# A transformer layer's projections and FFN in 16-bit parts, with the FFN's first layer paired by weight block

## The chip, the cores and the metric

The kernel runs on one core of one Trainium2 chip. The metric is the device time of that core in microseconds (us), from the start of the program to its end; three runs of the kernel before gave 2216.15, 2221.99 and 2224.67, median 2221.99. The core has five engines with queues of their own: TensorE (PE; its weight loads are listed apart as PEld), VectorE (DVE), ScalarE (ACT), GpSimd (POOL) and SyncE (SP, which issues the DMAs here).

## The reference

Sixteen sequences of 512 tokens with 256 features go through two attention blocks and, after each of them, the same FFN; every block has a layer norm in front and a residual sum behind. All of it is float32.

```python
def _L0_ffn_ref(x, w_gate, w_up, w_down):
    wg, wu, wd = (w.astype(x.dtype) * (1.0 / 127.0) for w in (w_gate, w_up, w_down))
    gate = jnp.einsum('bsd,hd->bsh', x, wg)
    up = jnp.einsum('bsd,hd->bsh', x, wu)
    h = jax.nn.silu(gate) * up
    return jnp.einsum('bsh,dh->bsd', h, wd)

x = L0_attn_a_x                                   # [16, 512, 256]
x = x + _L0_attn_a_ref(_layernorm(x), Wq, bq, Wk, bk, Wv, bv, Wo, bo)   # 16 heads, window +-32 and 4 global tokens
x = x + _L0_ffn_ref(_layernorm(x), w_gate, w_up, w_down)                # 256 -> 768 -> 256
x = x + _L0_attn_b_ref(_layernorm(x), Wqkv, Wout, bout)                 # rotary scores over unrotated sum, causal
x = x + _L0_ffn_ref(_layernorm(x), w_gate, w_up, w_down)
```

The FFN's weights are integers from -127 to 127, stored as int32.

## The kernel before

**Precision.** Float32 products are made of two parts: a value x is split into a high part and the rest, and a product takes high times high, high times low and low times high. The projections and the FFN hold both parts as float32r, which TensorE takes in one pass. The FFN's integer weights are exact in one part, so an FFN product has two passes, one for each part of x or of h. The scores of both attentions are made from float16 parts already (`src_a`, `src_b`, `pack_a`, `pack_b`).

**Order.** There is no scheduler. A table `AT` gives every step of a sequence a place on a common line, every sequence q is moved by 425 q places, and all steps are sorted into `STEPS`. Each engine walks through `STEPS` and issues its share in that order, so that up to four sequences are interleaved on it: attention A of one, the first FFN (F1) and attention B (PB, RB, B) of others, the second FFN (F2) of the oldest. A step that waits holds everything behind it on its engine. The period of a sequence is about 129 us.

**The steps that the change touches**, with the lines of the profile:
- `turn_x` (L1027) transposes the normalised x on PE. ScalarE copies the result to the high part of `xT` (L1185), VectorE subtracts to get the low part (L1433).
- `qk_step` (L1081) makes q and k, transposed: 6 matmuls of 128x128 weights and 512 columns a step, 48 a sequence over both attentions. `v_step` (L1004) makes v: 12 matmuls of 256 columns a step, 48 a sequence; here a block of x is the stationary operand.
- The FFN of half a sequence goes over three pairs of hidden blocks, so a step index i runs from 0 to 5. `ffn_up` (L1053) makes gate (G) and up (U), 8 matmuls of 256 columns each: high part of x first (4 of them), then low part (4). ScalarE takes the tanh (L1196), VectorE finishes gate (L1440), multiplies by up (L1446) and rounds the high part of h (L1457), GpSimd subtracts for the low part of h (L1576), and `ffn_down` (L1069) adds 8 matmuls of 256 columns into `d_bank`. Over both FFNs that is 192 matmuls of L1053 and 96 of L1069 a sequence.
- `o_step` (L1017) is the output projection. Its two parts `on_parts` are float32r and lie in the tile `xT[0]`.

**Start.** Weights are loaded, transposed on PE (L754), split by VectorE (L1269, L1270) or copied out of PSUM by ScalarE (L1227, L1230) into staging places, from which three DMAs bring the FFN's weights to `w_g`, `w_u` and `w_d`; PE and ScalarE wait for them (`w_raw`). VectorE finds the largest FFN weight; if it is over 2048, PE takes a branch of its program with true float32 matmuls, which these inputs do not take.

Of the kernel before, what the change touches and what calls it, by code (L numbers as in the profile page):

```python
# [13 lines left out]
HID = 768  # L14
# [8 lines left out]
EXACT = 2048.0  # L23
# [283 lines left out]
def build(nc, x_in, Wq, bq, Wk, bk, Wv, bv, Wo, bo, Wqkv, Wout, bout, w_gate, w_up, w_down,  # L307
# [7 lines left out]
    with ctx:  # L315
# [7 lines left out]
        wa_qk = [sb(f"wa_qk{i}", [P, KT, 2 * D], F32R) for i in range(2)]  # L323
        wa_v = [sb(f"wa_v{i}", [P, KT, D], F32R) for i in range(2)]
        wa_o = [sb(f"wa_o{i}", [P, KT, D], F32R) for i in range(2)]
        wb_qk = [sb(f"wb_qk{i}", [P, KT, 2 * D], F32R) for i in range(2)]
        wb_v = [sb(f"wb_v{i}", [P, KT, D], F32R) for i in range(2)]
        wb_o = [sb(f"wb_o{i}", [P, KT, D], F32R) for i in range(2)]
        w_g = sb("w_g", [P, KT, HID], F32R)
        w_u = sb("w_u", [P, KT, HID], F32R)  # L330
        w_d = sb("w_d", [P, FT, D], F32R)
# [30 lines left out]
        xT = [[sb(f"xT{b}{i}", [P, KT, S], F32R) for i in range(2)] for b in range(2)]  # L362
# [6 lines left out]
        w_top, w_top1 = newton[:, 0:1], newton[0:1, 1:2]  # L369
# [42 lines left out]
        w_raw = sem("w_raw")  # L412
# [88 lines left out]
        st_dT = stage(st_probs, FT * D, FT, D)  # L501
# [24 lines left out]
        def _(sp):  # L526
# [25 lines left out]
            for n, (dst, a) in enumerate(((w_g, st_gT), (w_u, st_uT), (w_d, st_dT))):  # L552
                sp.wait_ge(w_staged, (4, 8, 11)[n])
                sp.dma_start(dst[:, :, :].bitcast(F32), a).then_inc(w_raw, 16)
# [29 lines left out]
            def load_b(rotated, j, q):  # L584
# [5 lines left out]
                if j >= 2:  # L590
                    sp.wait_ge(scores, q * units + units // GROUPS * (j - 1))
                elif q:
                    sp.wait_ge(scores, (q - 1) * units + units // GROUPS * (j + 3))
                elif j == 0 and not rotated:
                    sp.wait_ge(wb_split, 1)
                load_pack(pack_b[:, j % 2, rotated], src_b[:, rotated], j, (u_packed, r_packed)[rotated][j])
# [132 lines left out]
        def _(pe):  # L729
# [28 lines left out]
            pe.wait_ge(w_flag, 1)  # L758
# [272 lines left out]
            def plain(a, exact):  # L1031
                return a if exact else a.bitcast(F32)

# [7 lines left out]
            def ffn_up(block, i, up, part, q, exact):  # L1041
# [4 lines left out]
                if part == 0:  # L1046
                    gu("GU"[up], i, block, q)
                for k in range(KT):
                    if i == 0 and not up:
                        x_there(block, part, k, q)  # L1050
                    for f in range(2):
                        c = (2 * pair + f) * P
                        last = pe.matmul(bank[:, f * D:(f + 1) * D], plain(w[:, k, c:c + P], exact),  # L1053
# [631 lines left out]
```

## Time and profile before

| what | value |
|---|---|
| runs of the kernel | 2216.15 to 2224.67 us, median 2221.99 |
| profiled execution, first to last instruction (span) | 2225.3 us |
| device time of the profiled execution | not given apart; the span is what the rows are taken from |
| PE busy, weight loads busy | 1928.7 us (87%), 1388.2 us (62%) |
| ACT, DVE, POOL busy | 65%, 64%, 36% |
| mean granted TensorE clock | 0.939 of 2.4 GHz |

PE is the busiest engine. A matmul's recorded length (281 ns for one of 256 columns) is longer than the step from one to the next, because they are pipelined; the steps are read from the starts in the timeline. The granted clock is 1.0 or 0.5, that is 2.4 or 1.2 GHz.

### The profile page before, as it was taken

What the parts mean: (1) busy time and instruction counts of PE and PEld (TensorE: products, weight loads), DVE (VectorE), ACT (ScalarE), POOL (GpSimd) and SP (SyncE); (2) the same over time, 40 slices, a digit from 0 to 9 for tenths busy, and PEclk for the clock granted to TensorE, in tenths of its full rate; (3) what the DMA queues carried; (4) which work ended last, traced back from release to release, by engine and by line L of the source; (5) the groups of instructions that cost most, each with busy time, mean ns of one, the idle gap of its engine ahead of it and who ended that gap; (6) DMA issues with size and microseconds to landing.
All of it is one profiled execution on the core that took longest, in us unless ns stands there. A gap on an engine that the chain in (4) does not pass through costs nothing.

```text
span 2225.3 us, 63347 instructions
## 1 busy us (share of the span) xinstructions
PE 1928.7 (87%) x25221; PEld 1388.2 (62%) x25221; DVE 1422.0 (64%) x2971; ACT 1444.9 (65%) x3580; POOL 796.1 (36%) x1131
## 2 busy tenths in 40 slices
PE   5677889889898989989898998989899898989786
PEld 4463657666675766667576666757666675756545
DVE  5363667576676757667675765767576676765624
ACT  1227676676867677676767767676776867677580
POOL 0023243433424343442434344243434424344431
PEclk7788999999999999999999999999999999999886
DMA  7224344252435335243533424353342434333321
GB/s 190 72 44 97 62 111 100 78 107 81 106 68 126 85 84 108 77 106 64 126 85 87 105 82 100 67 126 85 86 106 76 111 70 120 81 95 86 73 61 35
DMA packets 129636, 201.87 MB, mean 91 GB/s; under 512 B 26768, under 2 KB 60560, under 8 KB 129312
## 3 DMA queue, kind: packets, MB, share of 16 engines
q1 hardware_dynamic: 129344, 197.80, 37.1%
q8 instruction: 205, 3.36, 0.7%
q14 instruction: 87, 0.71, 0.1%
HBM read 67.87 MB, written 51.52 MB: 54 GB/s over the span
## 4 chain that ended last, share of the span: by engine, by line
PE 55%; ACT 17%; DVE 10%; issue 5%; SPq 5%; DMA 4%; POOL 4%; ACTq 0%; POOLq 0%; DVEq 0%
PE gu_bank L1053 15%; PE d_bank L1069 7%; ACT s_bank L1167 7%; PE gu_bank L1081 7%; SPq L575 4%; PE s_bank L984 4%; PE s_bank L948 4%; ACT probs_B L1157 3%; PE gu_bank L1017 3%; PE s_bank L814 2%; PE gu_bank L1027 2%; PE s_bank L969 2%; PE s_bank L822 2%; ACT probs_A L1150 2%; PE gu_bank L1004 2%
## 5 line engine op out<-in xcount | busy, mean ns | idle before, releaser
L1167 ACT ACTIVATE s_bank<-s_bank 128x512 f32<-128x512 f32 x1024 | 602.9, 591 | 123.3 <-PE s_bank L948 123.0
L1576 POOL TENSOR_TENSOR h<-tmp,h 128x512 fp32r<-128x512 f32 x192 | 252.0, 1312 | 451.6 <-DVE h L1457 451.6
L1157 ACT ACTIVATE probs_B<-s_bank 128x512 f32<-128x512 f32 x640 | 334.5, 610 | 48.5 <-PE s_bank L969 45.8
L1053 PE MATMUL gu_bank<-xT,w_g 128*128 128x256 f32 x1536 | 235.5, 298 | 25.1 <-DVE tmp L1440 21.1
L1053 PE MATMUL gu_bank<-xT,w_u 128*128 128x256 f32 x1536 | 241.3, 298 | 4.2 <-DVE tmp L1440 1.6
L1196 ACT ACTIVATE tmp<-gu_bank 128x512 f32<-128x512 f32 x192 | 114.6, 597 | 196.1 <-PE gu_bank L1053 188.5
L1053 PEld LDWEIGHTS gu_bank<-xT,w_g 128*128 128x128 f32 x1536 | 208.6, 199 | 52.9 <-DVE tmp L1440 35.8
L1053 PEld LDWEIGHTS gu_bank<-xT,w_u 128*128 128x128 f32 x1536 | 208.0, 198 | 37.6 <-issue 20.4
L1440 DVE SCALAR_TENSOR_TENSOR tmp<-tmp,gu_bank 128x512 f32<-128x512 f32 x192 | 130.6, 681 | 152.5 <-ACT tmp L1196 151.0
L1069 PE MATMUL d_bank<-w_d,h 128*128 128x256 f32 x1536 | 224.8, 288 | 3.3 <-POOL h L1576 3.3
L948 PE MATMUL s_bank<-pack_b 48*128 48x512 f16 x1024 | 180.4, 394 | 43.5 <-DVE o_raw L1361 19.9
L1593 POOL TENSOR_SCALAR_AFFINE_SELECT probs_B<-probs_B 128x256 f32<-128x256 f32 x512 | 194.3, 418 | 44.6 <-ACT probs_B L1157 44.3
L1069 PEld LDWEIGHTS d_bank<-w_d,h 128*128 128x128 f32 x1536 | 196.2, 188 | 17.0 <-issue 7.9
L1167 ACT ACTIVATION_READ_ACCUMULATOR s_bank<-s_bank 128x1 f32 x1024 | 196.7, 192 | 0.0
L1559 POOL TENSOR_TENSOR veps<-mv,eps 128x4 f32<-128x4 f32 x64 | 13.0, 203 | 483.7 <-DVE mv L1410 483.7
L1446 DVE TENSOR_TENSOR tmp<-tmp,gu_bank 128x512 f32<-128x512 f32 x192 | 132.0, 687 | 83.7 <-PE gu_bank L1053 81.8
L969 PE MATMUL s_bank<-pack_b 48*128 48x512 f16 (+3 forms) x1024 | 119.1, 314 | 71.9 <-DVE o_raw L1361 32.2
L1330 DVE TENSOR_REDUCE top<-s_bank 128x4 f32<-128x512 f32 x256 | 160.8, 681 | 5.6 <-PE s_bank L822 5.6
L984 PE MATMUL s_bank<-probs_B,v_aug_B 128*16 128x512 f32 (+3 forms) x2048 | 155.7, 446 | 2.6 <-POOL probs_B L1593 2.4
L1150 ACT ACTIVATE probs_A<-s_bank 128x512 f32<-128x512 f32 x256 | 133.4, 601 | 18.7 <-PE s_bank L822 17.8
L814 PE MATMUL s_bank<-band,eye_bf 64*64 64x512 bf16 x1024 | 111.2, 422 | 27.0 <-DMA pack_a<-src_a 12.9
L1581 POOL TENSOR_TENSOR tmp<-tmp,x 128x512 f32<-128x512 f32 x64 | 94.3, 1473 | 103.2 <-DVE x L1483 103.2
(140 smaller groups left out, 3303.5 us busy)
## 6 DMA issues: line engine op xcount, KB each, us to landing
pack_b<-src_b SPq DMA_DIRECT2D x768, 64.0 KB, 2.6
pack_a<-src_a SPq DMA_DIRECT2D x384, 64.0 KB, 2.3
x<-in_L_attn_a_x_dram SPq DMA_DIRECT2D x32, 512.0 KB, 4.9
o_scr_A<-o_raw SPq DMA_DIRECT2D x64, 256.0 KB, 2.4
o_scr_B<-o_raw SPq DMA_DIRECT2D x64, 256.0 KB, 2.4
xn<-o_scr_A SPq DMA_DIRECT2D x32, 256.0 KB
rden_on<-r_scr_A SPq DMA_DIRECT2D x32, 256.0 KB
x_scr<-x SPq DMA_DIRECT2D x16, 512.0 KB, 2.9
```

Source lines behind the costliest of these rows:

```text
L948: pe.matmul(score_bank("DP", n, q, e)[:, :], pack_b[r, j % 2, 0, 0, tile, t * P:(t + 1) * P], pack_b[r, j % 2, 0, 1, tile, :], start=True, ...
L969: last = pe.matmul(bank[e][:, c0:c0 + S - t * P], pack_b[r, j % 2, 1, 1, tile, t * P:(t + 1) * P], pack_b[r, j % 2, 1, 0, tile, t * P:S], ...
L984: last = pe.matmul(bank[32 * c:32 * c + DH, t * P:S], v_aug["B"][:, t, head(j, c), 0:DH], probs["B"][:, n, c0:c0 + S - t * P], start=t == ...
L1053: last = pe.matmul(bank[:, f * D:(f + 1) * D], plain(w[:, k, c:c + P], exact), plain(given[:, k, half * D:(half + 1) * D], exact), start=k ...
L1069: last = pe.matmul(bank[:, t, :], plain(h[part][:, i % 2, c:c + P], exact), plain(w_d[:, 2 * pair + f, :], exact), start=pair == 0 and f = ...
L1081: last = pe.matmul(bank[:, :], w_part[:, k, n * P:(n + 1) * P], given[part][:, k, :], start=k == 0 and i == 0, stop=k == KT - 1 and i == 2)
L1150: act.activation(dst, given, ACT.Exp, scale=SM_SCALE).then_inc(a_exp, 1)
L1157: act.activation(probs["B"][:, i, :], score_bank("NP", n // 2, q, n % 2)[:, :], ACT.Exp, scale=SM_SCALE)\
L1167: act.activation(bank[:, :], bank[:, :], ACT.Exp, scale=SM_SCALE, accum_out=den[:, 0, j, 2 * tile + e, t:t + 1]).then_inc(den_exp, 1)
L1330: dve.reduce_max(dst, a, AX.X).then_inc(a1_taken, 1)
L1576: pool.tensor_tensor(h[1][:, i % 2, :], tmp[:, i % 2, :], h[0][:, i % 2, :].bitcast(F32), ALU.subtract)\
L1593: ins = pool.affine_select(a, a, [[0, 2], [1, P]], ALU.is_ge, 0.0, base=0, channel_multiplier=-1)
```

## The change

All operands of the projections to q, k and v and of the FFN become 16-bit: `xT`, the attention weights `wa_qk`, `wa_v`, `wb_qk`, `wb_v` and `h` are float16 (these weights are multiplied by 16, the bias too, and the exponentials' scale is divided by 256), the FFN's weights are bfloat16. The number of matmuls and their shapes stay as they are. `on_parts` stays float32r and gets a tile of its own; its weights are divided by 16.

An FFN weight has up to three bfloat16 parts; the first alone is enough up to 256, the new bound of the branch. ScalarE writes each staged weight bank twice, to the first part and to the staging place; the three DMAs and `w_raw` are gone. GpSimd makes the other two parts in nine instructions behind its first step GM. PE's waiting branch, ScalarE's first step PBT1 and the first load of `pack_b` wait for them (`w_parts`).

h is scaled so that it fits float16: `hidden` multiplies by `h_scale`, `ffn_added` by `h_back`, both read from a tile of one value a partition; VectorE makes them at the start from the largest weight.

In the FFN's first layer a new function `ffn_up_paired` runs the steps from i = 1 on: for each weight block the product with the high part of x and the one with the low part follow each other.

```diff
-        w_g = sb("w_g", [P, KT, HID], F32R)
+        w_g = [sb(f"w_g{i}", [P, KT, HID], BF16) for i in range(W_PARTS)]
...
-        xT = [[sb(f"xT{b}{i}", [P, KT, S], F32R) for i in range(2)] for b in range(2)]
+        xT = [[sb(f"xT{b}{i}", [P, KT, S], F16) for i in range(2)] for b in range(2)]
...
-        on_parts = xT[0]
+        on_parts = [sb(f"on_part{i}", [P, KT, S], F32R) for i in range(2)]
...
-        h = [sb(f"h{i}", [P, 2, S], F32R) for i in range(2)]
+        h = [sb(f"h{i}", [P, 2, S], F16) for i in range(2)]
...
-            pe.transpose(gu_bank[0][0:1, 0:P], w_top, eye[:, :]).then_inc(w_turned, 1)
+            pe.transpose(gu_bank[0][:, 0:P], rden_on[:, 0, 0:P], eye[:, :]).then_inc(w_turned, 1)
             pe.wait_ge(w_flag, 3)
-            pe.wait_ge(w_raw, 48)
...
+            def ffn_up_paired(block, i, up, q, exact):
+                w, given = w_u if up else w_g, XT_OF[block]
+                half, pair = divmod(i, FT // 2)
+                bank = gu("GU"[up], i, block, q)
+                for k in range(KT):
+                    for f in range(2):
+                        c = (2 * pair + f) * P
+                        for n, w_part in enumerate(w[:1] if exact else w):
+                            for part in range(2):
+                                last = pe.matmul(bank[:, f * D:(f + 1) * D], w_part[:, k, c:c + P],
+                                                 given[part][:, k, half * D:(half + 1) * D],
...
-                    act.activation(st_dT[:, f:f + 2, :], bank.rearrange("p (k n) -> p k n", k=2), ACT.Copy).then_inc(w_staged, 1)
-            act.wait_ge(w_raw, 48)
+                    dst, given = [a[:, f:f + 2, :] for a in (w_d[0], st_dT)], bank.rearrange("p (k n) -> p k n", k=2)
+                act.activation(dst[0], given, ACT.Copy)
+                act.activation(dst[1], given, ACT.Copy).then_inc(w_staged, 1)
...
-                dve.tensor_tensor(t, t, gu_of("U", i, block, q)[:, :], ALU.mult).then_inc(gu_taken, 1)
+                dve.scalar_tensor_tensor(t, t, h_scale[:, 0:1], gu_of("U", i, block, q)[:, :], ALU.mult, ALU.mult).then_inc(gu_taken, 1)
...
-                pool.tensor_tensor(h[1][:, i % 2, :], tmp[:, i % 2, :], h[0][:, i % 2, :].bitcast(F32), ALU.subtract)\
+                pool.tensor_tensor(h[1][:, i % 2, :], tmp[:, i % 2, :], h[0][:, i % 2, :], ALU.subtract)\
...
+            def split_weights():
+                pool.wait_ge(w_staged, NBANKS - NSPLIT)
+                staged = (st_gT, st_uT, st_dT)
+                for n, (parts, rest) in enumerate(zip((w_g, w_u, w_d), staged)):
+                    pool.tensor_tensor(rest, rest, parts[0][:, :, :], ALU.subtract).then_inc(w_parts, 1)
+                    pool.wait_ge(w_parts, n * W_PARTS + 1)
+                    pool.tensor_copy(parts[1][:, :, :], rest).then_inc(w_parts, 1)
+                    pool.wait_ge(w_parts, n * W_PARTS + 2)
+                    pool.tensor_tensor(parts[2][:, :, :], rest, parts[1][:, :, :], ALU.subtract).then_inc(w_parts, 1)
```

On PE, the gate steps i = 1 and i = 2 of a first FFN, behind a pair of score matmuls; `xT10` is the high and `xT11` the low part of x. Before:

```order
L948 MATMUL s_bank0<-pack_b 128x512
L948 MATMUL s_bank1<-pack_b 128x512
L1053 MATMUL gu_bank0<-xT10,w_g 128x256 x4
L1053 MATMUL gu_bank0<-xT11,w_g 128x256 x4
L1053 MATMUL gu_bank1<-xT10,w_g 128x256 x4
L1053 MATMUL gu_bank1<-xT11,w_g 128x256 x4
```

Now:

```order
L952 MATMUL s_bank0<-pack_b 128x512
L952 MATMUL s_bank1<-pack_b 128x512
L1074 MATMUL gu_bank0<-xT10,w_g0 128x256
L1074 MATMUL gu_bank0<-xT11,w_g0 128x256
L1074 MATMUL gu_bank0<-xT10,w_g0 128x256
L1074 MATMUL gu_bank0<-xT11,w_g0 128x256
```

These four are half of the gate step, and the pattern goes on. The eight matmuls of a step are the same eight; two neighbours now have the same weights and write the same half of the bank.

On POOL, behind the start; GM of the first sequence is `ntop_glob`, the pair `veps`, `root` behind it is the layer norm of the second sequence. Before:

```order
L1608 TENSOR_TENSOR blocks<-src_a,strip 128x256
L1615 TENSOR_TENSOR ntop_glob<-ntopT,strip 32x64
L1559 TENSOR_TENSOR veps<-mv,eps 128x4
L1561 TENSOR_TENSOR root<-veps,minus_half 128x4
L1571 TENSOR_TENSOR x<-x,o_bias 128x256 x4
```

Now:

```order
L1645 TENSOR_TENSOR blocks<-src_a,strip 128x256
L1663 TENSOR_TENSOR ntop_glob<-ntopT,strip 32x64
L1653 TENSOR_TENSOR src_b<-src_b,w_g 128x1536
L1655 CAST w_g<-src_b 128x1536
L1657 TENSOR_TENSOR w_g<-src_b,w_g 128x1536
L1653 TENSOR_TENSOR src_b<-src_b,w_u 128x1536
L1655 CAST w_u<-src_b 128x1536
L1657 TENSOR_TENSOR w_u<-src_b,w_u 128x1536
L1653 TENSOR_TENSOR pack_b<-pack_b,w_d 128x1536
L1655 CAST w_d<-pack_b 128x1536
L1657 TENSOR_TENSOR w_d<-pack_b,w_d 128x1536
L1596 TENSOR_TENSOR veps<-mv,eps 128x4
```

Nine instructions of 1536 elements stand ahead of that layer norm, whose `root` VectorE waits for.

## Rows read from the trace of the kernel before

**Rows 1.** The page, busy time of each engine: us, share of the span, instructions.
```profile
PE 1928.7 (87%) x25221; PEld 1388.2 (62%) x25221; DVE 1422.0 (64%) x2971; ACT 1444.9 (65%) x3580; POOL 796.1 (36%) x1131
```

**Rows 2.** The page, the chain that ended last: shares by engine, then by line.
```profile
PE 55%; ACT 17%; DVE 10%; issue 5%; SPq 5%; DMA 4%; POOL 4%; ACTq 0%; POOLq 0%; DVEq 0%
PE gu_bank L1053 15%; PE d_bank L1069 7%; ACT s_bank L1167 7%; PE gu_bank L1081 7%; SPq L575 4%; PE s_bank L984 4%; PE s_bank L948 4%; ACT probs_B L1157 3%; PE gu_bank L1017 3%; PE s_bank L814 2%; PE gu_bank L1027 2%; PE s_bank L969 2%; PE s_bank L822 2%; ACT probs_A L1150 2%; PE gu_bank L1004 2%
```

**Rows 3.** Windows, one period: length, then each engine, clock, DMA share, GB/s.
```profile
1000.00:1128.60 128.60, 117.86 (x1573) 85.02 (x1573) 86.52 (x184) 89.38 (x222) 49.46 (x70) 0.96 0.38 93
```

**Rows 4.** Groups by line and shape, PE matmuls: busy us, mean ns, idle before.
```profile
L1053 PE MATMUL gu_bank<-xT,w_u 128*128 128x256 f32 x1536 | 241.3, 298 | 4.2 <-DVE tmp L1440 1.6 <-DVE tmp L1446 0.5
...
L1053 PE MATMUL gu_bank<-xT,w_g 128*128 128x256 f32 x1536 | 235.5, 298 | 25.1 <-DVE tmp L1440 21.1 <-DVE xT L1433 3.8
...
L1069 PE MATMUL d_bank<-w_d,h 128*128 128x256 f32 x1536 | 224.8, 288 | 3.3 <-POOL h L1576 3.3
...
L1081 PE MATMUL gu_bank<-xT,wa_qk 128*128 128x512 f32 x384 | 105.1, 418 | 5.0 <-DVE xT L1433 2.5 <-DVE src_a L1469 2.3
...
L1081 PE MATMUL gu_bank<-xT,wb_qk 128*128 128x512 f32 x384 | 104.0, 421 | 16.0 <-DVE tmp L1475 10.5 <-DVE xT L1433 5.4
```

**Rows 5.** Timeline of PE, one period: start, length, both in us, with the count.
```profile
1000.08 1.23 PE L1053 MATMUL gu_bank<-xT,w_g 128*128 128x256 f32 x8 [1.35 <-DVE tmp L1440]
1001.14 1.12 PE L1069 MATMUL d_bank<-w_d,h 128*128 128x256 f32 x8
1002.10 1.11 PE L1053 MATMUL gu_bank<-xT,w_u 128*128 128x256 f32 x8
...
1115.38 1.67 PE L1081 MATMUL gu_bank<-xT,wa_qk 128*128 128x512 f32 x6
```

**Rows 6.** Timeline of PE, 16-bit matmuls of 512 columns in runs of two and four.
```profile
1070.95 0.61 PE L1089 MATMUL gu_bank<-src_b,swap 128*128 128x512 f16 x2
...
2090.62 1.04 PE L1089 MATMUL gu_bank<-src_b,swap 128*128 128x512 f16 x4
```

**Rows 7.** Groups by line and shape, PE weight loads of 128 columns.
```profile
L1053 PEld LDWEIGHTS gu_bank<-xT,w_g 128*128 128x128 f32 x1536 | 208.6, 199 | 52.9 <-DVE tmp L1440 35.8 <-DVE xT L1433 9.7 <-issue 4.5
...
L841 PEld LDWEIGHTS s_bank<-blocks,src_a 128*128 128x128 f16 x384 | 10.7, 96 | 3.3 <-issue 2.9 <-ACT s_bank L1167 0.3
```

**Rows 8.** Timeline of PE, groups of four at the lower clock.
```profile
1101.10 1.05 PE L1053 MATMUL gu_bank<-xT,w_g 128*128 128x256 f32 x4
1101.95 1.05 PE L1053 MATMUL gu_bank<-xT,w_u 128*128 128x256 f32 x4
```

**Rows 9.** Windows around the lower clock in the same period.
```profile
1072.90:1076.30 3.40, 1.61 (x57) 0.75 (x38) 3.37 (x4) 1.77 (x4) 2.66 (x3) 1.00 0.53 114
1076.30:1079.80 3.50, 3.50 (x15) 2.77 (x16) 1.93 (x3) 2.35 (x6) 2.76 (x3) 0.51 0.49 142
1096.80:1103.60 6.80, 5.69 (x30) 3.93 (x26) 2.98 (x11) 4.91 (x13) 4.11 (x10) 0.50 0.55 91
```

**Rows 10.** Groups by line and shape, VectorE and GpSimd.
```profile
L1576 POOL TENSOR_TENSOR h<-tmp,h 128x512 fp32r<-128x512 f32 x192 | 252.0, 1312 | 451.6 <-DVE h L1457 451.6
...
L1446 DVE TENSOR_TENSOR tmp<-tmp,gu_bank 128x512 f32<-128x512 f32 x192 | 132.0, 687 | 83.7 <-PE gu_bank L1053 81.8
...
L1457 DVE CAST h<-tmp 128x512 fp32r<-128x512 f32 x192 | 88.6, 462 | 6.0 <-PE d_bank L1069 1.7
...
L1583 POOL TENSOR_TENSOR src_b<-tmp,src_b 128x512 f16<-128x512 f32 x64 | 74.5, 1165 | 89.0 <-ACT src_b L1220 89.0
...
L1469 DVE SCALAR_TENSOR_TENSOR src_a<-gu_bank,qk_bias,src_a 128x512 f16<-128x512 f32 x64 | 48.0, 750 | 75.0 <-ACT src_a L1206 75.0
```

**Rows 11.** Timeline of the fill, VectorE and GpSimd.
```profile
22.90 1.38 DVE L1404 BATCH_NORM_STATS2 stats<-x 128x6 f32<-128x256 f32 x4
...
65.29 0.28 POOL L1615 TENSOR_TENSOR ntop_glob<-ntopT,strip 32x64 f16<-32x64 f16 x1 [23.77 <-ACT ntopT L1172]
92.32 0.20 POOL L1559 TENSOR_TENSOR veps<-mv,eps 128x4 f32<-128x4 f32 x1 [26.75 <-DVE mv L1410]
```

More of the change, by code:

```diff
@@ L1047, in ffn_up @@
                     gu("GU"[up], i, block, q)
+                if not exact and part == 0 and i == 0 and FN[block, q] == 0:
+                    pe.wait_ge(w_parts, 3 * W_PARTS)
                 for k in range(KT):
@@ L1052, in ffn_up @@
                         c = (2 * pair + f) * P
[L1053 to L1055 removed]
+                        for n, w_part in enumerate(w[:1] if exact else w):
+                            last = pe.matmul(bank[:, f * D:(f + 1) * D], w_part[:, k, c:c + P],
+                                             given[:, k, half * D:(half + 1) * D],
+                                             start=k == 0 and part == 0 and f == 0 and n == 0, stop=k == KT - 1 and part == 1,
+                                             skip_group_check=True)
                 if part:
                     last.then_inc(gu_ready, 1)
+            def ffn_up_paired(block, i, up, q, exact):
[5 more added lines that the diff above has]
+                        c = (2 * pair + f) * P
+                        for n, w_part in enumerate(w[:1] if exact else w):
+                            for part in range(2):
+                                last = pe.matmul(bank[:, f * D:(f + 1) * D], w_part[:, k, c:c + P],
+                                                 given[part][:, k, half * D:(half + 1) * D],
+                                                 start=k == 0 and part == 0 and f == 0 and n == 0, stop=k == KT - 1 and part == 1,
+                                                 skip_group_check=True)
+                last.then_inc(gu_ready, 1)
             def ffn_down(block, i, q, exact):
@@ L1068, in ffn_down @@
                             c = f * D + t * P
-                            last = pe.matmul(bank[:, t, :], plain(h[part][:, i % 2, c:c + P], exact), plain(w_d[:, 2 * pair + f, :], exact),
-                                             start=pair == 0 and f == 0 and part == 0 and t == 0,
-                                             stop=pair == FT // 2 - 1 and f == 1 and part == 1, skip_group_check=True)
+                            for n, w_part in enumerate(w_d[:1] if exact else w_d):
+                                last = pe.matmul(bank[:, t, :], h[part][:, i % 2, c:c + P], w_part[:, 2 * pair + f, :],
+                                                 start=pair == 0 and f == 0 and part == 0 and t == 0 and n == 0,
+                                                 stop=pair == FT // 2 - 1 and f == 1 and part == 1, skip_group_check=True)
                 last.then_inc(d_ready if pair == FT // 2 - 1 else h_used, 1)
@@ L1117, in program @@
                                 ffn_up(block, n, up, part, q, exact)
-                    elif kind == "G" or kind == "U":
-                        for part in range(int(kind == "U" and n == 0), 2):
-                            ffn_up(block, n, int(kind == "U"), part, q, exact)
+                    elif (kind == "G" or kind == "U") and n:
+                        ffn_up_paired(block, n, int(kind == "U"), q, exact)
+                    elif kind == "U":
+                        ffn_up(block, n, 1, 1, q, exact)
                     elif kind == "FD":
@@ L1275, in split_bank @@
                 w, c = ((wa_qk, 0), (wa_qk, D), (wa_v, 0), (wa_o, 0))[n]
-                split([a[:, :, c:c + D] for a in w], bank).then_inc(w_taken, 1)
+                split([a[:, :, c:c + D] for a in w], bank, W_SCALE if n < 3 else 1.0 / W_SCALE).then_inc(w_taken, 1)
             def to_float(n):
```

84 lines of the change are left out of this document (50 added, 34 removed).

## The prediction

> **What bounds the kernel now.** I read the busy times, the chain, a window of one period, the groups by line and at last the timeline of PE, since a step between two matmuls can only be seen there. PE is busy for 87% of the span, ACT and DVE for about 65%, POOL for 36% [rows 1]; in a steady period of 128.6 us PE is busy for 117.9 us, the next engine, ACT, for 89.4 [rows 3]. The chain lies 55% on PE, and four lines that the change makes 16-bit hold 31% of it: L1053 15%, L1069 7%, L1081 7%, L1004 2% [rows 2]. So time taken off these matmuls is worth a large part of itself. No count of matmuls or columns changes; the question is what one of them costs with 16-bit operands.
>
> **What one step costs, float32r and 16-bit.** Eight float32r matmuls of 256 columns that follow others of their kind take 1002.10 - 1001.14 = 0.96 us, 0.120 us each, while the group before, which starts behind a wait of PE, takes 1.06 from start to start and lasts 1.23 us against 1.12 [rows 5]. 256 columns at 2.4 GHz are 0.107 us, so a following step has 0.012 over (I take 0.119), and a group that begins behind an idle PE or behind row-tiled matmuls has 0.10 to 0.11 us more once (I take 0.105): its first weight load isn't hidden. A recorded load lasts 199 ns in float32r and 96 in float16 [rows 7], a difference of 0.103. For 512 columns the six of L1081 last 1.67 us with one such entry; less a last matmul of 0.42 and the 0.105 that is 1.145 over five steps, 0.229; I take 0.230 [rows 4, 5].
>
> For 16 bits the nearest rows are L1089: float16, 128x128 weights, 512 columns. A run of two lasts 0.61 us, a run of four 1.04, so the third and fourth step are 0.215 us each [rows 6], 0.002 over the 0.213 of 512 columns. With the last matmul's 0.38 taken off a run of two, its only step is 0.23: an entry costs about 0.013 more, not 0.105. By these rows a following 16-bit step of 256 columns is 0.107 + 0.002 = 0.109 us. The bounds: nothing is gained in a following step if 0.012 stays as it is (0.119), and no more than 0.012 can be.
>
> The rule of the Trainium skill (TensorE: Matmul & The Clock Gate, section "Weight-path perf modes") is that the fast weight load is on for 128 columns and any type but FP32; the two lengths of rows 7 fit it. A rule of the same page speaks against the gain in following steps (section "The mechanism"): a load overlaps matmuls in flight only where the row group differs. By it every step of a float32r stream would carry its load, which the 0.120 us do not; taken for 16 bits it gives 0.107 + 0.013 = 0.120 and no gain there, which is rival B.
>
> **PE's sum.** A sequence has 192 matmuls of L1053, 96 of L1069 and 48 of L1004 with 256 columns, 48 of L1081 with 512. In the timeline of the period from 1000 to 1128.6 I count 24 entries on these lines, the first at 1000.08 [rows 5]. At the lower clock four matmuls take 1101.95 - 1101.10 = 0.85 us, 0.213 each, which is 256 columns at 1.2 GHz with nothing over [rows 8], so nothing is gained there; the granted clock of 0.96 [rows 3] means that 8% of the time is of that kind.
> - Following steps, 256 columns: (336 - 18) x 0.92 x 0.010 = 2.9 us.
> - Following steps, 512 columns: (48 - 6) x 0.92 x 0.015 = 0.6 us.
> - Entries: 24 x (0.105 - 0.013) = 2.2 us.
> Together 5.7 us a sequence, 91 us for 16. How much of it is on the path: the chain's 29% (15 + 7 + 7 [rows 2]) on L1053, L1069 and L1081 is 645 us of the 911 us that these lines are busy (241.3 + 235.5 + 224.8 + 105.1 + 104.0 [rows 4]), 0.71; L1004 lies on it for less. I take 0.68: 62 us. The rest is hidden already behind waits that others end.
>
> **The paired order.** It changes neither the count nor the shapes. The second load of a block is issued like the first: L1089 loads the same `swap` for both matmuls of its pair and its step is the 0.23 and 0.215 us of rows 6, so a repeated block is not skipped. Writing the same half of a bank twice in a row is what L1069 does now, four times over, at 0.120 [rows 5]. The value is 0; if the second load cost nothing at all, the most is the 0.002 us over the columns, 0.3 us a sequence.
>
> **VectorE and GpSimd.** `hidden` turns from a product of two tensors, 687 ns, to one with a factor per partition; L1469, that form, takes 750 [rows 10]. 63 ns x 192 is 12 us of DVE, and the same on `ffn_added` x64 is 4 us. Most lies beside PE's other work, since DVE has slack; what is on the path is bounded by 0 and 16, and the chain's 10% on DVE puts it near 2 to 3 us. The low part of h on POOL goes from 1312 ns to a form with float16 in and out, 1165 for L1583 [rows 10]: 147 ns shorter in the same chain of gate, up, h and down, 28 us of POOL, hidden for the most part and worth 1 us at most as POOL is 4% of the chain [rows 2]. The rounding of h (L1457, 462 ns) has one input and both ends in SBUF as before; I take no change, bounds -0.1 us and +0.2 us (the 687 of L1446) each, so at worst 43 us of DVE over 192, of which a tenth or two would show. The x parts cost ACT and DVE 10 ns more or less.
>
> **The start.** ScalarE copies each of its 11 banks twice, PE's last transposes and DVE's small steps wait behind, and DVE does four more operations before its first layer norm at 22.90 [rows 11]. The second copies fall partly into ScalarE's waits; I put the norm 2 us later (bounds 0 and 6). The three DMAs land before PE needs them in both. On GpSimd nine instructions of 1536 elements begin at 65.6 us, and the layer norm of the second sequence wants POOL at 92.32 [rows 11], 26.7 us later. The six subtractions at L1583's 2.27 ns an element are 3.5 us each, 21 us; the three casts lie between 1.4 us (half of that) and 3.9 (L1576's 2.56 ns), so 25 to 33 us in all: 0 to 6 us late, with the entry 2 us later than now. I take 2. Behind it stand VectorE's `root` step, PE's transposes and the projections of that sequence, all on the path in the fill.
>
> Sum: 2225.3 - 62 + 3 - 1 + 2 + 2 = 2169 for the profiled execution. Its span is 3 us over the median of 2222, so the median to come is **2166 us**, 2.5% less.
>
> **The rivals.**
> - A, all of the saving counts (chance 0.12). PE's 117.9 of 128.6 us a period speaks for it [rows 3]; against it stands that the table's order leaves PE waiting for ACT and DVE 10.7 us a period already. 2222 - 91 + 6 = 2137.
> - B, following steps gain nothing (0.13): the 16-bit weight switch costs 0.012 to 0.013 in every step, not just at an entry. For it: only the last steps of a run of four show 0.215, and a run of two, the common case of L1089, shows 0.23, and no row has bfloat16 weights with float16 columns. Left are the entries, 16 x 2.2 x 0.68 = 24: 2222 - 24 + 6 = 2204.
> - C, another chain takes over (0.12): the exponentials of attention B (L1167, 7%; L1157, 3%) and DVE's steps are the cover of each other in a fixed order; once PE has gained 2 us a period they end last. A third of the saving shows, 30 us: 2222 - 30 + 6 = 2198.
> - D, slower by the clock (0.05). Where PE is thinly used, the granted clock falls behind: 1.61 us busy of 3.4 at 1072.90, then 0.51, and once more 6.8 us at 0.50 [rows 9]. A PE that does the same work sooner waits more. 3.4 us of full matmuls at half clock lose 1.7 us of work. The 56 us of the forecast are gone with 33 more such stretches, two a sequence on top of today's three, and 2.5 or more a sequence make the kernel slower: four give 2166 + 16 x 4 x 1.7 = 2275. Against it: PE is busy for 92% of the period [rows 3], and most stretches are far from 1.61 of 3.4.
> - E, the change doesn't do what it says (0.03): 16-bit parts run through the array as float32r did, loads included, and 2222 + 6 = 2228.
>
> **How the numbers follow.** The forecast has 0.55, with 2145 to 2190 as its own range. What can be told from no change is 0.5%, 11 us. Faster: the forecast, A, most of C and 0.8 of B, 0.89. Within 0.5%: the rest of B and C, and E, 0.06. Slower: D, 0.05. The range from 2120 to 2207 takes in A, B and C and leaves out D and E.
>
> **What would show it.** In the trace after: weight loads of L1057, L1074, L1091 and the q, k, v lines at 96 ns instead of 188 to 199; groups of eight following others with 0.87 us from start to start instead of 0.96, and the same, not 0.10 more, behind a wait; `hidden` at 750; the low part of h at 1165; a period near 125 us; POOL's nine instructions ending between 91 and 99 us. The prediction is wrong if groups of eight keep 0.96 us (B), if the period keeps 128 us although they do not (C), or if the mean clock falls below 0.92 (D).

## The result, and the profile after

The changed kernel takes **2150.5 us** (median of 4 runs, 2144.4 to 2156.5) where the kernel before took 2219.1 beside it (4 runs, 2215.3 to 2224.7): a ratio of 0.9688, 95% interval 0.966 to 0.9715. That is 69 us or 3.1% less. The forecast was 2166, in a range of 2120 to 2207. The profiled execution has a span of 2154.8 us and a mean granted clock of 0.957 (0.939 before).

The page of the kernel after, busy time of each engine and the chain that ended last, answers to [rows 1, 2]:
```profile
PE 1819.5 (84%) x25221; PEld 1126.6 (52%) x25221; DVE 1427.9 (66%) x2978; ACT 1440.5 (67%) x3591; POOL 792.9 (37%) x1140
...
PE 43%; ACT 22%; DVE 16%; issue 6%; SPq 5%; POOL 4%; DMA 4%; ACTq 0%; POOLq 0%; DVEq 0%
```
PE gave up 109 us of busy time with the same 25,221 matmuls; DVE, ACT and POOL moved by less than 6 us each. The chain's share on PE fell from 55% to 43%, and ACT and DVE took what PE left.

The timeline of PE (start, length, count), the steps that [rows 5] showed:
```profile
1013.30 1.05 PE L1074 MATMUL gu_bank<-xT,w_u 128*128 128x256 f16 x8
1014.19 1.04 PE L1074 MATMUL gu_bank<-xT,w_g 128*128 128x256 f16 x8
1015.06 1.04 PE L1091 MATMUL d_bank<-w_d,h 128*128 128x256 bf16 x8
1015.93 1.04 PE L1074 MATMUL gu_bank<-xT,w_u 128*128 128x256 f16 x8
...
1084.95 1.47 PE L1103 MATMUL gu_bank<-xT,wa_qk 128*128 128x512 f16 x6
```
From 1014.19 to 1015.06 and on to 1015.93 is 0.87 us for eight, 0.109 each (0.96 before). The group at 1013.30 stands behind row-tiled matmuls (L952) and takes 0.89 to the next: such an entry costs 0.01 to 0.02, not 0.10. Six of 512 columns last 1.47 us, not 1.67.

Groups of weight loads, of VectorE and of GpSimd (busy us, mean ns), against [rows 7, 10]:
```profile
L1091 PEld LDWEIGHTS d_bank<-w_d,h 128*128 128x128 f16 x1536 | 142.5, 98 | 39.4 <-issue 12.8
L1074 PEld LDWEIGHTS gu_bank<-xT,w_g 128*128 128x128 bf16 x1280 | 121.4, 98 | 64.7 <-DVE tmp L1477 43.5
...
L1483 DVE SCALAR_TENSOR_TENSOR tmp<-tmp,h_scale,gu_bank 128x512 f32<-128x512 f32 x192 | 143.3, 746 | 69.4 <-PE gu_bank L1074 67.5
...
L1613 POOL TENSOR_TENSOR h<-tmp,h 128x512 f16<-128x512 f32 x192 | 227.7, 1186 | 436.0 <-DVE h L1494 436.0
```

Both kernels in windows of twelve periods, first before, then after (length, then busy us of PE, PEld, DVE, ACT and POOL, granted clock, DMA share, GB/s). Each window goes from the first layer norm of one sequence to that of the twelfth behind it:
```profile
324.90:1873.20 1548.30, 1401.56 (x18872) 1013.12 (x18872) 1051.97 (x2209) 1078.17 (x2674) 596.03 (x841) 0.97 0.39 93
```
```profile
322.50:1817.60 1495.10, 1322.11 (x18876) 822.15 (x18876) 1056.33 (x2209) 1072.78 (x2678) 576.84 (x840) 0.99 0.38 97
```
1548.3 / 12 = 129.0 us a period, 1495.1 / 12 = 124.6. So PE lost 6.6 us a period and the period 4.4, 53 us in all; the other 17 us of the 70.5 between the two profiled executions are in the fill and the drain. The clock rose from 0.97 to 0.99 in the steady part. By the trace's record of the granted clock a mean period before has 7.6 us at half clock (1.2 GHz), and 3.7 after. My sum had nothing for that.

### The profile page after: what moved, and what is told of

Its sections match the earlier page's. It is cut to its first block, busy times and chain, and to the rows that moved or that the text cites. A ratio compares the mean times of both kernels' runs of the same rounds, so it can differ in the third digit from the quotient of the medians.

```text
span 2154.8 us, 63371 instructions
## 1 busy us (share of the span) xinstructions
PE 1819.5 (84%) x25221; PEld 1126.6 (52%) x25221; DVE 1427.9 (66%) x2978; ACT 1440.5 (67%) x3591; POOL 792.9 (37%) x1140
## 4 chain that ended last, share of the span: by engine, by line
PE 43%; ACT 22%; DVE 16%; issue 6%; SPq 5%; POOL 4%; DMA 4%; ACTq 0%; POOLq 0%; DVEq 0%
PE gu_bank L1074 9%; ACT s_bank L1190 8%; PE gu_bank L1103 5%; PE d_bank L1091 4%; ACT probs_B L1180 4%; SPq L579 4%; PE s_bank L952 3%; ACT probs_A L1173 3%; DVE top L1364 3%; PE s_bank L988 2%; PE gu_bank L1057 2%; PE gu_bank L1021 2%; PE gu_bank L1031 2%; POOL tmp L1618 2%; PE s_bank L818 2%
## 5 line engine op out<-in xcount | busy, mean ns | idle before, releaser
L1613 POOL TENSOR_TENSOR h<-tmp,h 128x512 f16<-128x512 f32 x192 | 227.7, 1186 | 436.0 <-DVE h L1494 436.0
L952 PE MATMUL s_bank<-pack_b 48*128 48x512 f16 x1024 | 181.1, 392 | 44.4 <-DVE o_raw L1395 17.2
L1091 PE MATMUL d_bank<-w_d,h 128*128 128x256 bf16 x1536 | 199.9, 273 | 5.5 <-POOL h L1613 4.1
L1483 DVE SCALAR_TENSOR_TENSOR tmp<-tmp,h_scale,gu_bank 128x512 f32<-128x512 f32 x192 | 143.3, 746 | 69.4 <-PE gu_bank L1074 67.5
L1074 PE MATMUL gu_bank<-xT,w_g 128*128 128x256 f16 x1280 | 161.6, 274 | 29.2 <-DVE tmp L1477 29.2
L1074 PE MATMUL gu_bank<-xT,w_u 128*128 128x256 f16 x1280 | 167.8, 275 | 9.7 <-DVE src_a L1506 4.1
L1091 PEld LDWEIGHTS d_bank<-w_d,h 128*128 128x128 f16 x1536 | 142.5, 98 | 39.4 <-issue 12.8
L1074 PEld LDWEIGHTS gu_bank<-xT,w_g 128*128 128x128 bf16 x1280 | 121.4, 98 | 64.7 <-DVE tmp L1477 43.5
L1074 PEld LDWEIGHTS gu_bank<-xT,w_u 128*128 128x128 bf16 x1280 | 116.7, 98 | 60.1 <-issue 16.4
```

Source lines behind the costliest of these rows:

```text
L952: pe.matmul(score_bank("DP", n, q, e)[:, :], pack_b[r, j % 2, 0, 0, tile, t * P:(t + 1) * P], pack_b[r, j % 2, 0, 1, tile, :], start=True, ...
L1074: last = pe.matmul(bank[:, f * D:(f + 1) * D], w_part[:, k, c:c + P], given[part][:, k, half * D:(half + 1) * D], start=k == 0 and part == ...
L1091: last = pe.matmul(bank[:, t, :], h[part][:, i % 2, c:c + P], w_part[:, 2 * pair + f, :], start=pair == 0 and f == 0 and part == 0 and t = ...
L1483: dve.scalar_tensor_tensor(t, t, h_scale[:, 0:1], gu_of("U", i, block, q)[:, :], ALU.mult, ALU.mult).then_inc(gu_taken, 1)
L1613: pool.tensor_tensor(h[1][:, i % 2, :], tmp[:, i % 2, :], h[0][:, i % 2, :], ALU.subtract)\
```

## Experiments

Times are medians of five to twelve runs. Ratios are to the kernel before on the same chip, with 95% intervals. The changed kernel once more was the base of the first set.

> The changed kernel once more, as the base of this set. Expected by every theory: 2150 us, 0.969 of before.

Measured: 2150.3 us, 0.9668 (0.9649 to 0.9687), its steady periods 124.7 us with 4.4 at half clock. Two executions of one kernel differ there by 0.7 us a period, so the half-clock figures below, each from one execution, are no finer than that.

**The paired order, taken back.**
```diff
-                    elif (kind == "G" or kind == "U") and n:
-                        ffn_up_paired(block, n, int(kind == "U"), q, exact)
-                    elif kind == "U":
-                        ffn_up(block, n, 1, 1, q, exact)
+                    elif kind == "G" or kind == "U":
+                        for part in range(int(kind == "U" and n == 0), 2):
+                            ffn_up(block, n, int(kind == "U"), part, q, exact)
```


> The changed kernel with the old order of the first FFN layer: all products with the high part of x, then all with the low part; the same products, weights and parts. Theory 1 (the gain comes from 16-bit weight loads, 0.109 instead of 0.120 us a following product of 256 columns and 0.12 instead of 0.23 for the first behind a gap): a group of eight still goes 0.87 us from start to start, the time is that of the changed kernel within 0.3%, 2144 to 2157. Theory 2 (loading the same weights twice in a row makes the second load free or cheaper, and that is part of the gain): the products of the first layer behind one with other weights take 0.12 rather than 0.109; 160 of them are in a sequence, half with the same weights before them, so 80 x 0.011 = 0.9 us a sequence, 14 us in 16: 2160 to 2164; were pairing the whole gain, 2219.

Measured: 2154.7 us, 0.9692 (0.9672 to 0.9711). The timeline of PE of this kernel:
```profile
1019.42 1.05 PE L1057 MATMUL gu_bank<-xT,w_u 128*128 128x256 f16 x8
1020.30 1.04 PE L1057 MATMUL gu_bank<-xT,w_g 128*128 128x256 f16 x8
```
1.05 and 1.04 for eight, 0.88 from start to start, as in the changed kernel. The steps don't tell the orders apart, and the 4 us between the medians are inside the intervals. The time alone speaks for theory 1 (2144 to 2157) over theory 2 (2160 to 2164) only narrowly; the steps decide it.

**The paired order alone.** The kernel before with `ffn_up_paired`, float32r throughout:
```diff
...
+                        for part in range(2):
+                            last = pe.matmul(bank[:, f * D:(f + 1) * D], plain(w[:, k, c:c + P], exact),
+                                             plain(given[part][:, k, half * D:(half + 1) * D], exact),
...
```


> The kernel before with the new order of the first FFN layer alone: the products of one weight block with the high and the low part of x one behind the other, everything else float32r as before. Theory 1 (the gain is in 16-bit loads): groups of eight stay at 0.96 us, the time at 2222 within 0.3%. Theory 2 (loading the same block twice in a row is cheaper): 80 of the 160 products a sequence take 0.109 instead of 0.120, 0.9 us a sequence, 14 us in 16: 2208 or less.

Measured: 2220.6 us, 0.9996 (0.998 to 1.0011). Its PE timeline:
```profile
1000.28 1.22 PE L1068 MATMUL gu_bank<-xT,w_g 128*128 128x256 f32 x8 [1.35 <-DVE tmp L1456]
1001.33 1.12 PE L1084 MATMUL d_bank<-w_d,h 128*128 128x256 f32 x8
1002.29 1.12 PE L1068 MATMUL gu_bank<-xT,w_u 128*128 128x256 f32 x8
```
The rows are those of [rows 5] within 0.01 us, the entry behind a wait with its 0.10 too. The trace still has a load for every matmul (25,221 of each), so a block used twice in a row is loaded twice, at full price. Theory 2, which wanted 2208 or less, falls here.

**FFN alone in 16 bits.** Projections to q, k, v as before:
```diff
-        wa_qk = [sb(f"wa_qk{i}", [P, KT, 2 * D], F16) for i in range(2)]
+        wa_qk = [sb(f"wa_qk{i}", [P, KT, 2 * D], F32R) for i in range(2)]
...
-        XT_OF = {"F2": xT[0], "F1": xT[1], "PA": xT[1], "PB": xT[1], "VA": xT[1], "VB": xT[1]}
+        xP = [sb(f"xP{i}", [P, KT, S], F32R) for i in range(2)]
+        XT_OF = {"F2": xT[0], "F1": xT[1], "PA": xP, "PB": xP, "VA": xP, "VB": xP}
...
```


> The changed kernel with the projections to q, k and v on float32r parts again (their x in tiles of its own), the FFN and its paired order as changed. To fit in SBUF the second and third parts of the three FFN weights share one tile, which the branch taken here doesn't read. Theory 1, by products: the FFN has 288 of 360 changed products of a sequence and most entries, of 5.7 us that TensorE saves a sequence by my sum 4.5 are the FFN's; 80% of the gain of 70 us stays: 2160 to 2168. Rival (the projections are on the path, behind the layer norm, and the FFN is hidden under attention's copies and exponentials): less than half of the gain stays, 2190 to 2205.

Measured: 2171.9 us, 0.9784 (0.9765 to 0.9803): 48 us of the gain stay, 65 to 70%, and 21 to 26 hang on the projections. That is above the 2160 to 2168 of theory 1 and far below the rival's 2190. (The changed products of a sequence are 384, not the 360 that the expectation says.) PE's busy time, 1851.5 us, divides the same way: 32 of its 109 us are the projections'. I had counted 20%, and the timeline shows one thing I missed:
```profile
972.58 1.04 PE L1078 MATMUL gu_bank<-xT,w_g 128*128 128x256 f16 x8
973.42 1.69 PE L1012 MATMUL gu_bank<-wa_v,xP 128*128 128x256 f32 x12
```
A float32r group of twelve straight behind a 16-bit one lasts 1.69 us; behind a float32r one, as in the kernel with the paired order alone, it is 1.58, and behind row-tiled matmuls, in the kernel before, 1.68:
```profile
1003.88 1.22 PE L1068 MATMUL gu_bank<-xT,w_u 128*128 128x256 f32 x8
1004.93 1.58 PE L1004 MATMUL gu_bank<-wa_v,xT 128*128 128x256 f32 x12
```
```profile
1008.02 0.39 PE L948 MATMUL s_bank<-pack_b 48*128 48x512 f16 x2
1008.34 1.68 PE L1017 MATMUL gu_bank<-wa_o,xT 128*128 128x256 f32 x12
```
So a float32r load pays its 0.1 us at each change of type too, which mixing brings in. It is a small part of the 32 us: 26 of the groups that make v stand behind a 16-bit group in this trace, 26 x 0.11 = 3 us. The projections' x also no longer shares its tile with that of the first FFN here; the run doesn't separate that.

**The factors as numbers.**
```diff
-                dve.scalar_tensor_tensor(t, t, h_scale[:, 0:1], gu_of("U", i, block, q)[:, :], ALU.mult, ALU.mult).then_inc(gu_taken, 1)
+                dve.scalar_tensor_tensor(t, t, 2.0 ** -16, gu_of("U", i, block, q)[:, :], ALU.mult, ALU.mult).then_inc(gu_taken, 1)
...
-                dve.scalar_tensor_tensor(xs, tokens(d_bank), h_back[:, 0:1], xs, ALU.mult, ALU.add).then_inc(d_taken, 1)
+                dve.scalar_tensor_tensor(xs, tokens(d_bank), 0.5 * DEQUANT ** 3 * 2.0 ** 16, xs, ALU.mult, ALU.add).then_inc(d_taken, 1)
```


> The changed kernel with the two scale factors of the hidden values as numbers in the instruction (2^-16, and 2^16 times the old factor) in place of the column h_scale and h_back; right for weights up to 127. Theory A: the column as operand is what took the hidden product from 687 to 746 ns on VectorE; it returns to about 687. There are 12 a sequence, 12 x 0.06 = 0.7 us, 11 us in 16, of which VectorE's share of the chain (16%) up to all is felt: 2139 to 2149. Theory B: it is the second operation of the instruction (a product with a factor in place of a plain product of two tensors): 746 stays and so does the time, 2150.

Measured: 2154.1 us, 0.9694 (0.9669 to 0.9719). Its group of the hidden product:
```profile
L1483 DVE SCALAR_TENSOR_TENSOR tmp<-tmp,gu_bank 128x512 f32<-128x512 f32 x192 | 131.8, 686 | 66.6 <-PE gu_bank L1074 64.4 <-issue 0.4
```
Theory A has the duration right: the column as operand costs 60 ns. It has the time wrong: 11.5 us of VectorE are gone here, and 3.9 more in the 64 instructions that read `h_back` (47.8 to 43.9 us), and nothing is won. The row suggests why: before these products VectorE stands idle for 66.6 us, 64.4 of them until PE's `U` product is there, so a shorter product mostly waits longer.

**One part only.** Without ScalarE's second copies and GpSimd's nine instructions, which serve FFN weights above 256:
```diff
-                act.activation(dst[0], given, ACT.Copy)
-                act.activation(dst[1], given, ACT.Copy).then_inc(w_staged, 1)
+                act.activation(dst[0], given, ACT.Copy).then_inc(w_staged, 1)
...
-                for n, (parts, rest) in enumerate(zip((w_g, w_u, w_d), staged)):
-                    pool.tensor_tensor(rest, rest, parts[0][:, :, :], ALU.subtract).then_inc(w_parts, 1)
-                    pool.wait_ge(w_parts, n * W_PARTS + 1)
-                    pool.tensor_copy(parts[1][:, :, :], rest).then_inc(w_parts, 1)
-                    pool.wait_ge(w_parts, n * W_PARTS + 2)
-                    pool.tensor_tensor(parts[2][:, :, :], rest, parts[1][:, :, :], ALU.subtract).then_inc(w_parts, 1)
+                pool.sem_inc(w_parts, 3 * W_PARTS)
```


> The changed kernel without what serves only FFN weights above 256: ScalarE writes each staged bank once, not twice, and GpSimd's nine instructions that split the weights are left out (the branch that would read them is not taken here). Theory 1: the first layer norm starts 3 us earlier (25.9 back to 22.9), GpSimd's 23 us are under the wait for the second sequence's input: 2146 to 2148. Rival (GpSimd's 23 us hold up the masks and the second layer norm in the fill): 7 to 10 us less, 2140 to 2143.

Measured: 2151.1 us, 0.9675 (0.966 to 0.9691), the time of the changed kernel. GpSimd in the fill of the changed kernel:
```profile
67.78 3.09 POOL L1653 TENSOR_TENSOR src_b<-src_b,w_g 128x1536 f32<-128x1536 f32 x1
70.93 1.46 POOL L1655 CAST w_g<-src_b 128x1536 bf16<-128x1536 f32 x1
72.47 3.09 POOL L1657 TENSOR_TENSOR w_g<-src_b,w_g 128x1536 bf16<-128x1536 f32 x1
...
88.01 3.09 POOL L1657 TENSOR_TENSOR w_d<-pack_b,w_d 128x1536 bf16<-128x1536 f32 x1
96.20 0.20 POOL L1596 TENSOR_TENSOR veps<-mv,eps 128x4 f32<-128x4 f32 x1 [5.10 <-DVE mv L1444]
```
The nine end at 91.1, and GpSimd then still waits 5.1 us for the second sequence's norm: they delay nothing there.

Theory 1's step did not come. The first layer norm begins at 24.74 us, not at 22.9; in the changed kernel it was 25.86 in the first profiled execution, and 24.70 in the one that was run again:
```profile
24.74 1.40 DVE L1437 BATCH_NORM_STATS2 stats<-x 128x6 f32<-128x256 f32 x4
```
```profile
25.86 1.40 DVE L1438 BATCH_NORM_STATS2 stats<-x 128x6 f32<-128x256 f32 x4
```
```profile
24.70 1.40 DVE L1438 BATCH_NORM_STATS2 stats<-x 128x6 f32<-128x256 f32 x4
```
So two executions of one kernel differ by 1.2 us at this place, the second copies show no cost in it, and the run doesn't tell what a norm at 22.9 would be worth.

**TensorE's time given back.** 64 products with zeros a sequence:
```diff
+                        if k == 0:
+                            pe.matmul(bank[:, f * D:(f + 1) * D], nought[:, :], given[0][:, k, half * D:(half + 1) * D],
+                                      start=False, stop=False, skip_group_check=True)
...
+                        if f:
+                            pe.matmul(bank[:, t, :], nought[:, :], w_d[0][:, 2 * pair, :], start=False, stop=False, skip_group_check=True)
```


> The changed kernel with 64 more products of 256 columns a sequence in the FFN: two in each group of the first layer behind the first, two in each of the second, with a weight block of zeros that adds nothing to the sum. TensorE gets back 64 x 0.109 = 7.0 us a sequence, about what the change took from it (116.6 to 109.8 us of busy time a period). Theory 1 (TensorE's time is what the period is made of, with a share of 0.64 as 6.9 us less gave 4.4): 7.0 x 0.64 x 16 = 72 us more, 2222; between 2205 and 2250. Theory 3 (a good part of the gain is the granted clock, which holds higher when TensorE computes rather than waits for loads): busy zeros keep the clock, so it would be at 0.96 or above, and the time at 2150 to 2190.

Measured: 2225.0 us, 1.0014 (1.0005 to 1.0023). Twelve of its periods:
```profile
325.50:1871.90 1546.40, 1396.27 (x19646) 899.88 (x19648) 1059.19 (x2209) 1078.76 (x2679) 577.06 (x840) 0.98 0.37 94
```
PE is as busy as in the kernel before (1396 against 1402) and the period is its period, 128.9 us. 64 x 0.109 x 16 = 112 us of PE made the kernel 75 us slower: 0.67 of a us for each. (By the windows PE is busy for 6.2 us a period more than in the changed kernel and the period is 4.3 longer, 0.69.) PE's time is the cause of the period, by a share near the one I took. The clock is not behind it: there are 4.6 us at half clock a period, against 3.7 and 4.4 in the two executions of the changed kernel.

**The clock.** To see what half clock costs, products with zeros go where PE waits over a microsecond. They add nothing to a bank that is open or free:
```diff
+IDLE = {("NP", 18, "B"): 10, ("DP", 0, "B"): 10, ("NP", 1, "B"): 10, ("NP", 4, "B"): 10, ("G", 4, "F2"): 12}
...
+            def noughts(count):
+                if taken[0]:
+                    pe.wait_ge(d_taken, taken[0])
+                for _ in range(count):
+                    pe.matmul(d_bank[:, 0:D], nought[:, 0:P], nought[:, :], start=False, stop=False, skip_group_check=True)
...
```
In the kernel before:

> The kernel before with the same products of zeros in the same five places, no other change. Theory 3: half clock goes from 7.6 us a period to 3 or less, 4.6 x 0.35 = 1.6 us a period, 22 us in 14: about 2200. If the clock costs nothing: 2222.

Measured: 2199.6 us, 0.9915 (0.9894 to 0.9935). Its timeline of PE ahead of attention B's scores (L1069 are the zeros, and a wait is left behind them), and twelve of its periods:
```profile
1061.45 1.27 PE L1069 MATMUL d_bank<-nought 128*128 128x256 f16 x10
1064.10 0.39 PE L951 MATMUL s_bank<-pack_b 48*128 48x512 f16 x2 [1.39 <-DMA pack_b<-src_b]
```
```profile
322.80:1846.70 1523.90, 1438.40 (x19496) 1044.77 (x19496) 1053.96 (x2209) 1077.07 (x2672) 595.61 (x840) 1.00 0.40 95
```
The clock is 1.00 through all twelve periods, and 52 products more a sequence make the kernel 19 us faster. The period is 127.0 us, 2.0 shorter; with 7.6 us at half clock gone that is 0.27 us for each, the cost of the zeros included. The forecast of 2200 came out by two misses that cancel: more half clock went than the 4.6 us, and each was worth less than the 0.35.

In the changed kernel:

> The changed kernel with products of zeros where TensorE waits over 1.2 us in each period (behind the values of attention A, in two places ahead of attention B's scores, ahead of the fifth gate product of the second FFN): 52 of 256 columns a sequence, which add nothing to a sum that is open or free. Theory 3 (a part of the gain is the granted clock: over the periods of six traces each us at half clock goes with 0.26 to 0.45 us of period, and the changed kernel's mean period has 3.7 us of it where the kernel before has 7.6): the stretches at half clock go to 1 us a period or less, 2.7 x 0.35 = 0.9 us a period, 14 us in all: 2133 to 2142. Against it (the clock falls elsewhere, or costs nothing): 2150. If the products of zeros don't end within the waits, 52 x 0.109 = 5.7 us a sequence at 0.64: up to 2208.

Measured: 2145.1 us, 0.967 (0.9649 to 0.9691). Twelve periods:
```profile
314.90:1800.50 1485.60, 1376.83 (x19502) 871.74 (x19500) 1057.40 (x2209) 1073.64 (x2677) 577.12 (x840) 1.00 0.39 97
```
The clock holds here too and the period falls to 123.8 us, 0.8 less; the ratio of the runs shows no gain (0.967 against 0.9668). What half clock was left to the changed kernel is worth 0 to 10 us.

The two filled kernels are the comparison of the change at an equal clock in the steady periods: PE is busy for (1438.40 - 1376.83) / 12 = 5.1 us a period less and the period is 3.2 us shorter, a share of 0.62.

With the clock out of the way in both, the paired order was compared once more (the edit above on this kernel):

> The changed kernel with the products of zeros in the five waits and with the old order of the first FFN layer. Without half clock in the steady periods the order is compared by itself. The order is worth nothing: 0.967 of before, as with the products of zeros alone, 2145, period 123.8. The order is worth the 4 us by which the unpaired kernel stood above the changed one: 2149, 0.969, period 124.1.

Measured: 2147.6 us, 0.9676 (0.966 to 0.9692), against 0.967 with the pairs: the order is worth nothing that these runs can measure. They can't rule out the 4 us either. Twelve of its periods:
```profile
314.70:1803.20 1488.50, 1378.96 (x19503) 872.37 (x19500) 1059.56 (x2209) 1073.93 (x2677) 576.91 (x840) 1.00 0.39 97
```
That is 124.0 us a period, the figure put down for an order that is worth 4 us. In the other two pairs of kernels the unpaired one has the longer period as well (124.9 against 124.6 and 124.7, 129.0 against 128.8), each from one execution, while the steps are the same.

**The output projections in 16 bits**, a version that might beat both:
```diff
-        wa_o = [sb(f"wa_o{i}", [P, KT, D], F32R) for i in range(2)]
+        wa_o = [sb(f"wa_o{i}", [P, KT, D], F16) for i in range(2)]
...
-        on_parts = [sb(f"on_part{i}", [P, KT, S], F32R) for i in range(2)]
+        on_parts = [sb(f"on_part{i}", [P, KT, S], F16) for i in range(2)]
...
```


> The changed kernel with the output projections on 16-bit parts too (weights and both parts of the attention output f16; 48 products of 256 columns a sequence). Theory 1: following products go from 0.117 to 0.109 us and the first behind a gap from 0.223 to 0.12; 48 x 0.008 = 0.4 us and four entries x 0.1 = 0.4 us a sequence, 13 us in 16, 60 to 80% of it on the path: 2140 to 2143. Theory 3 (beyond that a less busy TensorE shifts the clock): the mean granted clock moves from 0.957 and the time by more than these 10 us. Rival: the output projection waits for the outputs that come back by DMA, so its products are hidden: 2150.

Measured: 2140.4 us, 0.9635 (0.9609 to 0.966), 10 us under the changed kernel at the medians. Twelve periods:
```profile
319.80:1804.50 1484.70, 1304.16 (x18876) 800.49 (x18876) 1054.61 (x2209) 1075.25 (x2678) 577.13 (x841) 0.99 0.39 98
```
Theory 1's number came out: PE is 18 us less busy in twelve periods and the period 123.7 us (124.6). Only 1.4 us a period are left at half clock, so a part of the gain may be theory 3's mechanism; this run doesn't divide them.

> The changed kernel with the output projections on 16-bit parts and with the products of zeros in the five waits. If both effects stand and add: 2140 less 3 to 10 (the output projections in 16 bits alone had left only 1.4 us of half clock a period), 2130 to 2137. If the gain of the 16-bit output projections was the clock alone: the same time as with the products of zeros alone.

Measured: 2139.5 us, 0.9635 (0.9615 to 0.9655), its clock 1.00 in all twelve periods at 123.4 us each. Against the filled kernel without these parts (0.967, 123.8 us) 16-bit output projections are 0.35% or some 7 us faster at equal clock, at the edge of what the intervals can tell. The effects don't add (2130 to 2137 did not come): filling adds nothing to them. The best version is the changed kernel with 16-bit output projections, 0.9635.

## Why the prediction was right, step by step

- **Steps of TensorE.** The size of each step held: 0.109 us following, 0.01 to 0.02 instead of 0.105 at an entry, loads of 98 ns. Their sum was somewhat high: 5.7 us a sequence forecast, 5.1 a period measured at an equal clock (82 us in 16, not 91); the 6.6 of the two kernels as they are has the clock in it. Rival B kept following steps at 0.120; they went to 0.109. The rule of the section "The mechanism" of the Trainium skill's page "TensorE: Matmul & The Clock Gate", that a load overlaps running matmuls only where the row group differs, doesn't hold for these rows: full-array matmuls step at 0.109 us, each with a load of 98 ns of its own. The same section of the Trainium skill also lets a load be pulled ahead into a background weight buffer, and that fits them.
- **What they are worth.** Forecast: 62 us, 0.68 of 91. With the clock at 1.00 in the steady periods of both, 2199.6 less 2145.1 is 54.5 us, everything else of the change included: 0.60 of the 91 forecast, 0.66 of the 82 measured. Giving PE its time back priced it at 0.67. The share taken from the chain was good to a tenth.
- **The projections.** Their part was under-counted (near 30%, not 20%, a little of it the mixing of types that only the kernel with the FFN alone has), and that of the FFN over-counted.
- **VectorE +3.** The durations held (746 for 750), the price did not: with the durations taken back nothing is won. A share of the chain is not the price of an instruction.
- **GpSimd -1, splitting and start +4.** The low part of h takes 1186, not 1165 ns. The nine instructions took 23.3 us where I had 25 to 33: a subtraction is 3.09 us, not 3.5, and half of 3.5 is 1.75, not the 1.4 that I wrote (the casts took 1.46). They hold up nothing. The first norm came 3.0 us later (25.86 against 22.90) in the first trace and 1.8 (24.70) in the second; what that is worth no run shows, since the kernel with one part has it at 24.74.
- **Paired order 0.** Right as far as the runs can tell, tested three times; up to 4 us stay possible.
- **What was missing** is the clock, worth 69 less 54.5, some 14 us, and by the intervals of the three ratios in it anything from 5 to 25. In the fill and the drain the two filled kernels are not quite alike (0.89 and 0.94 before, 0.88 and 0.92 with the change), so this division is an estimate. Rival D had the mechanism, waits of PE that go with a falling clock, but the wrong sign: a PE that is less busy (88% of a period against 91%) had less half clock, not more.
- **The number.** 2166 was 16 us high: 3 us because the kernel before ran at 2219.1 beside it and not at 2222, the rest the clock. That the remainder fits so well, 56 us forecast and 54.5 measured at an equal clock, is partly luck: PE's 62 us were some 7 too many, and the 6 us that VectorE, GpSimd, splitting and start should have cost did not show.

Rivals A and C are out by the time, B by the steps, E by both. **Open** is why the changed kernel falls to half clock less often. The waits matter, since filling them took all of it out of the steady periods. But a wait alone doesn't decide. The changed kernel has the same stretch in two periods (window, busy times and clock):
```profile
901.80:905.20 3.40, 2.10 (x22) 1.15 (x19) 2.49 (x9) 2.92 (x6) 0.94 (x1) 1.00 0.26 87
905.20:908.60 3.40, 3.40 (x47) 1.86 (x46) 2.12 (x3) 1.70 (x4) 3.35 (x6) 0.50 0.41 159
```
```profile
1528.10:1531.50 3.40, 2.10 (x19) 1.25 (x17) 2.86 (x9) 3.10 (x7) 0.89 (x2) 1.00 0.39 114
1531.50:1652.70 121.20, 106.72 (x1561) 66.89 (x1561) 86.06 (x180) 87.55 (x220) 47.74 (x70) 1.00 0.38 96
```
PE is busy for 2.10 us of 3.4 in both; the clock halves behind the first, and behind the second none of the period is at half clock. A weak hint is the kernel with 64 zeros a sequence: the same period as before, but with 16-bit loads, and 4.6 us at half clock where 7.6 were. That would make the unhidden float32r loads a part of it. But the kernel with the paired order alone, float32r throughout, has 6.3, so one execution says little, and no run tests it by itself.

## What to carry to other kernels

Read the step between two matmuls from start to start in the timeline, once behind a neighbour of the same kind and once behind a wait or another tiling; the difference between the two is what the load that isn't hidden costs, and here 16 bits took it away (0.105 to 0.01 or 0.02 us). Price a saving on the engine that bounds the kernel by putting the same time back as dead work: it told the share to within a tenth, while the share of the chain on a side engine promised 2 to 3 us for VectorE's 60 ns, which were worth nothing. And where the granted clock is under 1.00 in the steady part, fill the bounding engine's long waits with products of zeros: it shows what the clock costs, and may pay by itself (0.85% here before the change, nothing measurable after it).

## What the hardware showed that was not expected

- A float32r weight load of 128 columns is hidden behind a float32r product of the same shape, but not behind a 16-bit one or row-tiled matmuls: there the first step is 0.10 us longer (twelve take 1.69 and 1.68 us, against 1.58).
- On VectorE a column as factor instead of a number costs 60 ns on 128x512 with one input from PSUM (746 against 686, and 747 against 686 in the second place).
- GpSimd takes 3.09 us for a subtraction of 128x1536 and 1.46 for the cast to bfloat16, 2.01 and 0.95 ns an element; at 128x512 from float32 and float16 it is 2.3 ns an element.
- Taking a microsecond at half clock out of the steady part gave this kernel about 0.27 us (2.03 us of period for 7.6), what the zeros themselves cost included. By the steps of a stream without waits I would estimate 0.44 to 0.49: 256 columns take 0.213 us at half clock in [rows 8], and 0.119 in float32r or 0.109 in 16 bits at full clock.
